# Layer 1 of the first batch over five groups of both rows at once, with two low parts of W1 made by GpSimd

## The chip, the cores and the metric

The kernel runs on one core of one Trainium2 chip. The metric is the device time of one execution in microseconds; lower is better. Engines are named as in the profile: PE is TensorE's matmul, PEld its weight load, DVE VectorE, ACT ScalarE, POOL GpSimd, SP SyncE.

## The reference

Two layers on x of shape (8, 256, 1024), each added to its input. Layer 0 has a full matrix of its own for every batch element, made from a mask; layer 1 has one matrix and a LoRA pair picked by an id.

```python
# layer 0
output = jnp.einsum('bsi,oi->bso', hidden_states, W) + b
sign = (2 * mask - 1).astype(hidden_states.dtype)
diff = jnp.einsum('bsi,bio->bso', hidden_states, sign)
x = x + output + diff * coeff[:, None, None]
# layer 1, SCALING = 2
base_out = jnp.einsum('bti,oi->bto', x, W) + b
lora_h = jnp.einsum('bti,bir->btr', x, lora_As[adapter_mapping])
lora_out = jnp.einsum('btr,bro->bto', lora_h, lora_Bs[adapter_mapping])
x = x + base_out + lora_out * SCALING
```

## The kernel before

**Precision.** Every float32 operand is split into a high part (rounded to float32r by a ScalarE copy) and a low part (the rest, by a subtraction on VectorE or GpSimd), and each product is made of three matmuls: high x high, high x low, low x high. The residual is folded into the weights: GpSimd adds the identity to the diagonal block of W0 and W1 (`w1_diagonal`, L229).

**Batches and tiles.** The eight batch elements follow each other. The contraction of 1024 is cut into KT = 8 blocks k of 128; x and y are held transposed, in four pairs of blocks (`g` in 0 to 3, XG = 4). Layer 0 of batch b writes y in four PSUM banks `y_ps0` to `y_ps3`: for each k, 16 matmuls with the high part of that block of weights (`layer0_high`, L286) and 8 with the low part (`layer0_low`, L296). The weights of block k are made anew for each batch: VectorE adds W0 and 2c times the mask (`weights_sum`, L551), ScalarE takes the high part (`weights_high`, L408), VectorE the low one (`weights_low`, L560). They lie in rings of four blocks, so that mask k + 4 is loaded only after the low part of block k is made.

**Layer 1.** y is split by `y_high` (L426) and `y_low` (L583) out of PSUM. The output's 256 tokens are two rows `s` of 128, and its 1024 columns plus the R = 16 columns of LoRA's A three groups `g` of 352, 344 and 344 columns, one PSUM bank `z_ps0` to `z_ps2` each. `products(b, s, g, k)` (L310) is three matmuls of one group and one block. W1 is split once, in the first batch, by `w1_high` (L414) and `w1_low` (L571); `w1_lo` lies where `w1_raw` lay. Group 0 of a row also yields h, the product with A: `h_high` (L432) and `h_low` (L591) read it, `turn_h` (L344) transposes it on TensorE, `h_copy` (L437) takes it back, and `close_group` (L353) adds h times B and the bias b1 to a group with one matmul. The rows of b1 are split and put into `b_stack` by GpSimd and two DMAs of its queue (L248 to L254); B's low part is `lora_b_low` (L243). `z_copy` (L444) takes a group out of PSUM, and `store` sends a row.

**Order.** There is no planner: each engine's order is written out by hand, and an instruction waits on counting semaphores. `z_done` counts z copies and tells TensorE which bank is free. For batch 0, before: TensorE does `layer0(0)`; then `layer1_first()`, row 0's three groups block by block, each block as soon as its low part is made (`w1_lo_done >= k + 1`); then row 1's group 0 in `y_ps3`, then row 1's group 1. Row 1's group 2 of every batch is left to `layer1_last`, after layer 0 of the next batch. VectorE alternates `w1_low` of eight blocks with `y_low` of four pairs. ScalarE's x block g of batch 0 is split after the weights of block 2g - 1. On SP's queue all loads stand in one order: W0 and mask by turns, x, W1 with LoRA's A and B, then batch 1's x and masks. GpSimd does the diagonals of W0, the b1 rows, the diagonals of W1 (with `lora_a_low(0)`, L237, after the second), then `lora_b_low(0)`.

Of the kernel before, what the change touches and what calls it, by code (L numbers as in the profile page):

```python
# [17 lines left out]
def cond_residual_two_layers(nc, x, coeff, slot_ids, mask, w0, b0, w1, b1, lora_a, lora_b, out):  # L18
# [17 lines left out]
    with ExitStack() as ctx:  # L36
# [69 lines left out]
        w1_hi_done = sem("w1_hi_done")  # L106
        w1_lo_done = sem("w1_lo_done")
        x_hi_done = sem("x_hi_done")
        x_lo_done = sem("x_lo_done")
# [18 lines left out]
        def mask_entry(b, k):  # L128

            return KT * b + k  # L130

        def need(eng, s, n):
# [21 lines left out]
        def z_bank(b, s, g):  # L154

            return y_ps[XG - 1] if (b, s, g) == (0, 1, 0) else z_ps[g]

# [4 lines left out]
        def _(sp):  # L162
# [18 lines left out]
            def load_lora(b):  # L181
# [32 lines left out]
        def _(pool):  # L214
# [30 lines left out]

            pool.wait_ge(w0_diag, KT)
            pool.wait_ge(b1_in, 16)
# [19 lines left out]
        def _(pe):  # L267
            def warm_up(n):
                for _ in range(n):
                    pe.transpose(t_ps[:, 0:P], ident[:], ident[:])  # L270

            def layer0_high(b, k):

                pe.wait_ge(x_lo_done, XG * b + k // PAIR + 1)
                for o in range(KT):
                    if o % HT == 0 and (o == 0 or (b, k) == (0, 0)):
                        pe.wait_ge(wc_hi_done, parts(b, k, o // HT))
                    if k == 0 and o % PAIR == 0:
                        need(pe, y_lo_done, KT * (b - 1) + o + PAIR)
                    if b == 1 and k == 0 and o == KT - PAIR:  # L280

                        pe.wait_ge(z_done, NG + 1)
                    ys = y_ps[o // PAIR][:, (o % PAIR) * T:(o % PAIR + 1) * T]
                    w = wc_hi[:, k % RING, o * P:(o + 1) * P]
                    for n in range(2):
                        pe.matmul(ys, w, x_two[:, k, n, :], start=(k == 0 and o % PAIR == 0 and n == 0),  # L286
                                  stop=False, skip_group_check=True)

            def layer0_low(b, k):

                for o in range(KT):
                    if o % HT == 0 and (o == 0 or (b, k) == (0, 0)):
# [23 lines left out]

            def layer1_first():

                pe.wait_ge(lora_lo_done, 1)
                for k in range(KT):  # L320
                    pe.wait_ge(w1_lo_done, k + 1)
                    pe.wait_ge(y_lo_done, k + 1)
                    for g in range(NG):
                        products(0, 0, g, k)

            def layer1_group(b, s, g, ks=range(KT)):
                if ks[0] == 0:

                    if (b, s, g) != (0, 1, 0):
                        need(pe, z_done, NG * (ST * b + s - 1) + g + 1)  # L330
# [15 lines left out]
            def close_group(b, s, g):  # L346
# [3 lines left out]
                if g == 0:  # L350
# [4 lines left out]
                          start=False, stop=True, skip_group_check=True).then_inc(z_full, 1)  # L355

            def layer1(b):

                for s in range(ST):
                    if b > 0:  # L360
                        layer1_group(b, s, 0)
                        layer1_group(b, s, 1, range(HT))
                        turn_h(b, s)
                        layer1_group(b, s, 1, range(HT, KT))
                        close_group(b, s, 0)
                        close_group(b, s, 1)
                    elif s == 0:
                        layer1_first()
                        layer1_group(0, 1, 0, range(HT))
                        turn_h(0, 0)  # L370
                        layer1_group(0, 1, 0, range(HT, KT))
                        close_group(0, 0, 0)
                        close_group(0, 0, 1)
                    if s == 0 and b > 0:
                        layer1_group(b, 0, 2)
                    if s == 0:
                        close_group(b, 0, 2)
                    if s == 1 and b == 0:
                        layer1_group(0, 1, 1, range(HT))
                        turn_h(0, 1)  # L380
                        layer1_group(0, 1, 1, range(HT, KT))
                        close_group(0, 1, 0)
                        close_group(0, 1, 1)

# [7 lines left out]
            layer0(0)  # L392
            layer1(0)
            for b in range(1, NB):
# [7 lines left out]
        def _(act):  # L402
# [36 lines left out]
            def z_copy(b, s, g):  # L439
                act.wait_ge(z_full, NG * (ST * b + s) + g + 1)  # L440
                if g == 0:
# [5 lines left out]
            def store(b, s, g0=0, g1=NG):  # L447
                act.wait_ge(z_done, NG * (ST * b + s) + g1)
                lo, hi = max(EDGES[g0] - R, 0), EDGES[g1] - R
                act.dma_start(out_v[b, s][:, lo:hi], z_rows[:, s, lo:hi]).then_inc(z_out[s], 16)  # L450

            def lora_a_high(b):
                act.wait_ge(a_in, 16 * (b + 1))
                if b > 0:

                    act.wait_ge(z_full, NG * (ST * b - 1) + 1)
                act.activation(w1_hi[:, :, 0:R], a_raw[:], ACT.Copy).then_inc(lora_hi_done, 1)  # L457
# [25 lines left out]
            y_high(0, 0)  # L483
            w1_high(2)
            y_high(0, 1)
            w1_high(3)
            w1_high(4)
            y_high(0, 2)
            w1_high(5)
            y_high(0, 3)  # L490
            w1_high(6)
            w1_high(7)
            lora_b_high(0)


            for b in range(1, NB + 1):
                a = b - 1
                if a > 0:
                    for g in range(XG):
                        y_high(a, g)  # L500
                if b < NB:
                    for g in range(XG):
                        x_high(b, g)
                if a > 0:
                    z_copy(a - 1, 1, 2)
                    store(a - 1, 1)
                    lora_b_high(a)
                h_high(a, 0)
# [29 lines left out]
        def _(dve):  # L538
# [58 lines left out]


            weights_sum(0, 0, 0)
            x_low(0, 0)  # L600
            weights_sum(0, 0, 1)
            weights_low(0, 0, 0)
            weights_low(0, 0, 1)
            weights_sum(0, 1)
            for k in range(1, KT):
                if k % PAIR == 1 and k < KT - 1:
                    x_low(0, k // PAIR + 1)
                if k < KT - 1:
                    weights_sum(0, k + 1)
                weights_low(0, k)  # L610
            w1_low(0)
# [13 lines left out]
            for b in range(1, NB):  # L625
                a = b - 1
                if a > 0:
                    for g in range(XG):
                        y_low(a, g)
                for g in range(XG):  # L630
# [42 lines left out]
```

## Time and profile before

| what | value |
| --- | --- |
| median of 3 runs | 404.98 us (404.46 to 405.29) |
| the profiled execution's own time | 407.7 us |
| its span, first to last instruction | 405.9 us |
| mean granted TensorE clock | 0.992 |
| busy: PE, PEld | 389.5 us (96%), 385.7 us (95%) |
| busy: DVE, ACT, POOL | 221.0 us, 159.7 us, 39.5 us |
| DMA | 61.80 MB, mean 152 GB/s |

Busy times are of the profiled execution, which took 2.7 us more than the median; 1.8 us of it lie outside the span. An engine that is not the bottleneck may be idle at no cost, so the table alone doesn't tell what sets the time.

### The profile page before, as it was taken

The page shows a single profiled execution, that of the slowest core. Times are in us where ns is not written, and L with a number is a line of the kernel's source. Part 1 is how long each engine was busy: PE and PEld are TensorE (multiplying, and loading weights), DVE is VectorE, ACT ScalarE, POOL GpSimd, SP SyncE. Part 2 cuts the span into 40 slices and gives each one's busy share as a digit, 9 for nine tenths or more (in the row PEclk, how much of TensorE's full clock was granted, in tenths as well). Part 3 has the DMA queues.
Part 4 walks back from the last instruction along what each step waited for, and adds up shares of the span by engine and source line. Part 5 has one row for each costly group of instructions (what it writes and reads, how often), then busy time and mean ns, then how long its engine had stood idle before and what let it go on. Part 6 is the DMA issues. An engine that isn't in the chain of part 4 may idle for free.

```text
span 405.9 us, 6725 instructions
## 1 busy us (share of the span) xinstructions
PE 389.5 (96%) x2782; PEld 385.7 (95%) x2782; DVE 221.0 (54%) x267; ACT 159.7 (39%) x283; POOL 39.5 (10%) x44
## 2 busy tenths in 40 slices
PE   7798797999999999999999999999999999999997
PEld 7688696999999999999999999999999999999996
DVE  2797977616756277525746177553775258460300
ACT  3446834306433353316424064334534164241311
POOL 1236300002000020000200020000200001000200
PEclk9999988999999999999999999999999999999999
DMA  7999808531565126640365216650266413500111
GB/s 250 407 382 333 328 27 271 196 110 53 180 205 174 45 79 207 209 161 33 110 221 199 95 53 191 197 200 16 80 207 219 152 52 111 177 2 2 52 53 52
DMA packets 21056, 61.80 MB, mean 152 GB/s; under 512 B 2698, under 2 KB 3874, under 8 KB 21026
## 3 DMA queue, kind: packets, MB, share of 16 engines
q1 hardware_dynamic: 18064, 52.70, 38.3%
q10 hardware_dynamic: 2898, 8.66, 6.0%
q8 instruction: 22, 0.36, 0.4%
q14 instruction: 8, 0.07, 0.0%
q0 software_dynamic: 64, 0.01, 0.0%
HBM read 52.97 MB, written 8.39 MB: 151 GB/s over the span
## 4 chain that ended last, share of the span: by engine, by line
PE 85%; DMA 4%; DVE 3%; POOL 2%; issue 2%; ACT 1%; SPq 1%; ACTq 0%; DVEq 0%; POOLq 0%
PE z_ps L310 42%; PE y_ps L286 26%; PE y_ps L296 13%; DMA ring<-in_mask 2%; DVE w_lo L571 2%; DMA w_t<-in_w 2%; PE z_ps L353 2%; PE y_ps L310 1%; DVE y_two L583 1%; ACT wc_hi L408 1%; PE t_ps L344 0%; POOL w_t L227 0%; POOL w_raw L232 0%; ACT w_hi L414 0%; POOL b_parts L250 0%
## 5 line engine op out<-in xcount | busy, mean ns | idle before, releaser
L310 PE MATMUL z_ps<-w_hi,y_two 128*128 128x344 f32 (+1 forms) x752 | 189.2, 327 | 4.4 <-DVE w_lo L571 2.7
L310 PEld LDWEIGHTS z_ps<-w_hi,y_two 128*128 128x128 f32 x752 | 133.7, 191 | 6.3 <-DVE w_lo L571 3.6
L286 PE MATMUL y_ps<-x_two,wc_hi 128*128 128x256 f32 x1024 | 133.8, 284 | 2.3 <-ACT wc_hi L408 1.7
L286 PEld LDWEIGHTS y_ps<-x_two,wc_hi 128*128 128x128 f32 x1024 | 127.9, 192 | 3.0 <-issue 1.7
L310 PE MATMUL z_ps<-w_lo,y_two 128*128 128x344 f32 (+1 forms) x376 | 121.8, 324 | 0.0
L560 DVE SCALAR_TENSOR_TENSOR wc_lo<-ring,coeff_neg,wc_hi 128x1024 fp32r<-128x1024 f32 (+1 forms) x65 | 83.1, 1279 | 50.0 <-ACT wc_hi L408 49.2
L408 ACT ACTIVATE wc_hi<-ring,coeff_neg 128x1024 fp32r<-128x1024 f32 (+1 forms) x65 | 74.0, 1138 | 65.6 <-PE y_ps L296 53.6
L551 DVE SCALAR_TENSOR_TENSOR ring<-ring,coeff_two,w_t 128x1024 f32<-128x1024 int32 (+1 forms) x65 | 83.1, 1286 | 6.6 <-DMA ring<-in_mask 6.1
L296 PE MATMUL y_ps<-x_two,wc_lo 128*128 128x256 f32 x512 | 72.2, 284 | 2.5 <-DVE wc_lo L560 2.5
L310 PEld LDWEIGHTS z_ps<-w_lo,y_two 128*128 128x128 f32 x376 | 71.8, 191 | 0.0
L296 PEld LDWEIGHTS y_ps<-x_two,wc_lo 128*128 128x128 f32 x512 | 66.0, 192 | 3.1 <-DVE wc_lo L560 3.1
L583 DVE SCALAR_TENSOR_TENSOR y_two<-y_ps,b_cols,y_two 128x256 fp32r<-128x256 f32 x64 | 26.1, 476 | 65.1 <-ACT y_two L426 65.1
L426 ACT ACTIVATE y_two<-y_ps,b_cols 128x256 fp32r<-128x256 f32 x64 | 24.5, 488 | 67.5 <-PE y_ps L296 67.5
L243 POOL TENSOR_TENSOR b_stack<-b_raw,b_stack 32x1024 fp32r<-32x1024 f32 x8 | 19.1, 2386 | 199.3 <-ACT b_stack L462 199.3
L444 ACT ACTIVATE z_rows<-z_ps 128x344 f32<-128x344 f32 (+1 forms) x47 | 20.0, 459 | 33.7 <-PE z_ps L353 33.7
L591 DVE SCALAR_TENSOR_TENSOR h_rows<-z_ps,h_rows 128x16 fp32r<-128x16 f32 x30 | 3.8, 169 | 47.2 <-ACT h_rows L432 47.2
L576 DVE TENSOR_TENSOR x_two<-x_raw,x_two 128x512 fp32r<-128x512 f32 x32 | 20.2, 684 | 3.2 <-ACT x_two L420 3.2
L432 ACT ACTIVATE h_rows<-z_ps 128x16 fp32r<-128x16 f32 x30 | 3.9, 181 | 39.5 <-PE z_ps L310 39.5
L420 ACT ACTIVATE x_two<-x_raw 128x512 fp32r<-128x512 f32 x32 | 18.1, 665 | 2.7 <-DMA x_raw<-in_x 2.7
L237 POOL TENSOR_TENSOR w_lo<-a_raw,w_hi 128x128 fp32r<-128x128 f32 x8 | 3.7, 462 | 120.0 <-ACT w_hi L457 120.0
L437 ACT ACTIVATE h_stack<-t_ps 66x128 fp32r<-66x128 f32 x16 | 4.4, 273 | 22.3 <-PE t_ps L344 22.3
L571 DVE TENSOR_TENSOR w_lo<-w_raw,w_hi 128x1024 fp32r<-128x1024 f32 x8 | 12.0, 1528 | 1.5 <-ACT w_hi L414 1.5
(35 smaller groups left out, 91.3 us busy)
## 6 DMA issues: line engine op xcount, KB each, us to landing
ring<-in_mask SPq DMA_DIRECT2D x63, 512.0 KB, 3.3
x_raw<-in_x SPq DMA_DIRECT2D x31, 256.0 KB, 5.5
out<-z_rows ACTq DMA_DIRECT2D x15, 512.0 KB, 3.9
w_raw<-in_w SPq DMA_DIRECT2D x8, 512.0 KB, 10.2
w_t<-in_w SPq DMA_DIRECT2D x7, 512.0 KB, 9.1
b_raw<-in_lora_b SPq DMA_DIRECT2D x8, 256.0 KB, 3.5
w_t<-in_w SPq DMA_DIRECT2D x2, 256.0 KB, 4.4
ring<-in_mask SPq DMA_DIRECT2D x2, 256.0 KB, 5.9
```

The costliest lines, as they stand in the source:

```text
L243: pool.tensor_tensor(b_stack[2 * R:LR, :], b_raw[2 * R:LR, :], b_stack[2 * R:LR, :].bitcast(F32), ALU.subtract).then_inc(lora_lo_done, 1)
L286: pe.matmul(ys, w, x_two[:, k, n, :], start=(k == 0 and o % PAIR == 0 and n == 0), stop=False, skip_group_check=True)
L296: ins = pe.matmul(ys, w, x_two[:, k, 0, :], start=False, stop=(k == KT - 1), skip_group_check=True)
L310: ins = pe.matmul(z_bank(b, s, g)[:, 0:EDGES[g + 1] - EDGES[g]], ys[:, k, s * P:(s + 1) * P], w[:, k, EDGES[g]:EDGES[g + 1]], start=(k == ...
L408: act.activation(wc_hi[:, k % RING, lo:hi], sums[:, e % RING, lo:hi], ACT.Identity, bias=coeff_neg[:, b:b + 1]).then_inc(wc_hi_done, 1)
L426: act.activation(y_two[:, b % 2, 0, o, :], y_ps[g][:, (o % PAIR) * T:(o % PAIR + 1) * T], ACT.Identity, bias=b0_cols[:, o:o + 1]).then_inc ...
L444: act.activation(z_rows[:, s, EDGES[g] + lo - R:EDGES[g + 1] - R], z_bank(b, s, g)[:, lo:EDGES[g + 1] - EDGES[g]], ACT.Copy).then_inc(z_do ...
L551: dve.scalar_tensor_tensor(out=sums[:, e % RING, lo:hi], in0=ring[:, e % RING, lo:hi], scalar=coeff_two[:, b:b + 1], in1=w0_t[:, k, lo:hi] ...
L560: dve.scalar_tensor_tensor(out=wc_lo[:, k % RING, lo:hi], in0=sums[:, mask_entry(b, k) % RING, lo:hi], scalar=coeff_neg[:, b:b + 1], in1=w ...
L571: dve.tensor_tensor(w1_lo[:, k, R:R + D], w1_raw[:, k, R:R + D], w1_hi[:, k, R:R + D].bitcast(F32), ALU.subtract).then_inc(w1_lo_done, 1)
L576: dve.tensor_tensor(x_two[:, PAIR * g:PAIR * (g + 1), 1, :], x_raw[:, PAIR * g:PAIR * (g + 1), :], x_two[:, PAIR * g:PAIR * (g + 1), 0, :] ...
L583: dve.scalar_tensor_tensor(out=y_two[:, b % 2, 1, o, :], in0=y_ps[g][:, (o % PAIR) * T:(o % PAIR + 1) * T], scalar=b0_cols[:, o:o + 1], in ...
```

## The change

For batch 0 alone, layer 1 now runs over five groups at once: (0,0), (0,1), (0,2), (1,0) and (1,1), written (row, group). Group (1,0) is held in `y_ps0` and (1,1) in `y_ps1`. They start when `y_low` has read those banks. `layer1_first` does blocks 0 and 1 of four groups, then of the fifth, blocks 2 to 5 of all five, and 6 and 7 group by group; both turns of h stand between the last products of (0,2), and the five closes come at the end, in the order (0,0), (1,0), (1,1), (0,1), (0,2), which `z_place` numbers. Layer 0 of batch 1 begins with output blocks 4 to 7 in its first weight block.

GpSimd makes `w1_lo` of blocks 4 and 7 (`SIDE`), counted by a semaphore of its own; VectorE makes the other six. GpSimd's b1 work moves behind these. SP's queue loads x block 0 first, which ScalarE's queue did before. ScalarE and VectorE have their orders of batch 0 written anew. From batch 2 on the orders are as they were.

```diff
+        SIDE = (4, 7)
+        def w1_split(eng, k):
+            eng.wait_ge(w1_lo_done, k + 1 - sum(j <= k for j in SIDE))
+            need(eng, w1_lo_side, sum(j <= k for j in SIDE))
...
         def z_bank(b, s, g):
-            return y_ps[XG - 1] if (b, s, g) == (0, 1, 0) else z_ps[g]
+            return y_ps[g] if b == 0 and s == 1 and g < 2 else z_ps[g]
+        def z_place(b, s, g):
+            if b == 0:
+                return ((0, 0), (1, 0), (1, 1), (0, 1), (0, 2), (1, 2)).index((s, g)) + 1
+            return NG * (ST * b + s) + g + 1
...
+            load_x(0, 0)
             sp.dma_start(w0_t[:, 0, 0:HALF], w0[0, :, 0:HALF]).then_inc(w0_first, 16)
...
-            pool.wait_ge(w0_diag, KT)
+            w1_diagonal(0)
+            w1_diagonal(1)
+            lora_a_low(0)
+            for k in range(2, KT):
+                w1_diagonal(k)
+            for k in SIDE:
+                pool.wait_ge(w1_hi_done, k + 1)
+                pool.wait_ge(w1_diag, k + 1)
+                pool.tensor_tensor(w1_lo[:, k, R:R + D], w1_raw[:, k, R:R + D],
+                                   w1_hi[:, k, R:R + D].bitcast(F32), ALU.subtract).then_inc(w1_lo_side, 1)
             pool.wait_ge(b1_in, 16)
...
-            w1_diagonal(0)
-            w1_diagonal(1)
-            lora_a_low(0)
-            for k in range(2, KT):
-                w1_diagonal(k)
             lora_b_low(0)
...
+            def outputs(b, k):
+                return [*range(HT, KT), *range(HT)] if (b, k) == (1, 0) else [*range(KT)]
...
-                    if b == 1 and k == 0 and o == KT - PAIR:
-                        pe.wait_ge(z_done, NG + 1)
+                    if b == 1 and k == 0 and o % PAIR == 0 and o < HT:
+                        pe.wait_ge(z_done, z_place(0, 1, o // PAIR))
...
+            def first_products(s, g, ks):
+                for k in ks:
+                    w1_split(pe, k)
+                    pe.wait_ge(y_lo_done, max(k + 1, PAIR * (g + 1) if s == 1 else 0))
+                    products(0, s, g, k)
...
+            def layer1_first():
+                pe.wait_ge(lora_lo_done, 1)
+                for k in range(PAIR):
+                    for s, g in ((0, 0), (0, 1), (0, 2), (1, 0)):
+                        first_products(s, g, [k])
+                first_products(1, 1, range(PAIR))
+                for k in range(PAIR, KT - PAIR):
+                    for s, g in ((0, 0), (0, 1), (0, 2), (1, 0), (1, 1)):
+                        first_products(s, g, [k])
+                for s in range(ST):
+                    first_products(s, 0, range(KT - PAIR, KT))
+                for s in range(ST):
+                    first_products(s, 1, range(KT - PAIR, KT))
+                turn_h(0, 0)
+                first_products(0, 2, [KT - PAIR])
+                turn_h(0, 1)
+                first_products(0, 2, [KT - 1])
+                for s, g in ((0, 0), (1, 0), (1, 1), (0, 1), (0, 2)):
+                    close_group(0, s, g)
...
-            act.dma_start(x_raw[:, 0:PAIR, :], x[0, :, 0:PAIR, :]).then_inc(x_in[0], 16)
...
+            x_high(0, 0)
             for k in range(KT):
-                if k % PAIR == 0:
-                    x_high(0, k // PAIR)
+                if k % PAIR == 1 and k < KT - 1:
+                    x_high(0, k // PAIR + 1)
                 weights_high(0, k)
             w1_high(0)
-            w1_high(1)
             lora_a_high(0)
             act.wait_ge(b0_in, 16)
...
+            for g in range(XG):
+                y_high(0, g)
+                w1_high(g + 1)
+            for k in range(XG + 1, KT):
+                w1_high(k)
             lora_b_high(0)
...
+            for g in range(XG):
+                x_high(1, g)
+            h_high(0, 0)
+            h_high(0, 1)
+            weights_high(1, 0)
+            h_copy(0, 0)
+            h_copy(0, 1)
+            z_copy(0, 0, 0)
+            z_copy(0, 1, 0)
+            z_copy(0, 1, 1)
+            weights_high(1, 1)
+            z_copy(0, 0, 1)
+            z_copy(0, 0, 2)
+            store(0, 0)
+            lora_a_high(1)
+            for k in range(2, KT):
+                weights_high(1, k)
...
+            x_low(0, 0)
             weights_sum(0, 0, 0)
-            x_low(0, 0)
             weights_sum(0, 0, 1)
             weights_low(0, 0, 0)
             weights_low(0, 0, 1)
             weights_sum(0, 1)
+            x_low(0, 1)
             for k in range(1, KT):
...
             w1_low(2)
             w1_low(3)
             y_low(0, 2)
-            w1_low(4)
+            y_low(0, 3)
             w1_low(5)
-            y_low(0, 3)
             w1_low(6)
-            w1_low(7)
...
+            x_low(1, 0)
+            weights_sum(1, 0)
+            h_low(0, 0)
+            h_low(0, 1)
+            for k in range(KT):
+                if k + 1 < XG:
+                    x_low(1, k + 1)
+                step(1, k)
```

## Rows read from the trace of the kernel before

**Rows 1.** The page, parts 1 and 2: busy time, and tenths by slice.
```profile
PE 389.5 (96%) x2782; PEld 385.7 (95%) x2782; DVE 221.0 (54%) x267; ACT 159.7 (39%) x283; POOL 39.5 (10%) x44
...
PE   7798797999999999999999999999999999999997
...
PEclk9999988999999999999999999999999999999999
```
**Rows 2.** The chain of waits in order of time: start us, us, what.
```profile
63.04 0.27 ACT h_rows L432 x2
...
69.10 1.92 PE y_ps L286 x16
71.02 0.96 PE y_ps L296 x8
...
92.14 3.81 PE z_ps L310 x24
...
386.68 0.31 PE z_ps L353 x2
```
**Rows 3.** Timeline of TensorE: start us, us, line, tiles; idle before and releaser.
```profile
8.59 1.22 PE L286 MATMUL y_ps<-x_two,wc_hi 128*128 128x256 f32 x8 [0.66 <-DVE x_two L576]
...
24.04 1.22 PE L296 MATMUL y_ps<-x_two,wc_lo 128*128 128x256 f32 x8 [0.70 <-DVE wc_lo L560]
...
30.34 1.21 PE L296 MATMUL y_ps<-x_two,wc_lo 128*128 128x256 f32 x8 [0.28 <-DVE wc_lo L560]
...
38.38 0.40 PE L310 MATMUL z_ps<-w_hi,y_two 128*128 128x352 f32 x1 [1.07 <-DVE y_two L583]
...
50.46 0.44 PE L310 MATMUL z_ps<-w_hi,y_two 128*128 128x352 f32 x1 [1.93 <-DVE w_lo L571]
...
65.09 0.27 PE L344 MATMUL t_ps<-ident,h_rows 128*66 128x128 f32 x1 [2.81 <-issue]
...
68.90 2.12 PE L286 MATMUL y_ps<-x_two,wc_hi 128*128 128x256 f32 x16
```
**Rows 4.** Stretches of TensorE: stretch us, length, busy, granted clock, DMA share, GB/s.
```profile
36.00:38.00 2.00, 1.31 (x11) 1.00 1.06 400
...
52.00:53.00 1.00, 1.00 (x6) 0.50 0.00 0
...
38.30:68.90 30.60, 23.55 (x120) 0.89 0.62 219
```
**Rows 5.** Timeline of VectorE.
```profile
20.70 0.69 DVE L576 TENSOR_TENSOR x_two<-x_raw,x_two 128x512 fp32r<-128x512 f32 x1 [0.54 <-ACT x_two L420]
...
26.99 0.69 DVE L576 TENSOR_TENSOR x_two<-x_raw,x_two 128x512 fp32r<-128x512 f32 x1 [0.61 <-ACT x_two L420]
...
46.41 0.87 DVE L583 SCALAR_TENSOR_TENSOR y_two<-y_ps,b_cols,y_two 128x256 fp32r<-128x256 f32 x2
...
47.19 3.21 DVE L571 TENSOR_TENSOR w_lo<-w_raw,w_hi 128x1024 fp32r<-128x1024 f32 x1
```
**Rows 6.** Timeline of ScalarE.
```profile
39.64 2.00 ACT L414 ACTIVATE w_hi<-w_raw 128x1024 fp32r<-128x1024 f32 x2
41.53 0.84 ACT L426 ACTIVATE y_two<-y_ps,b_cols 128x256 fp32r<-128x256 f32 x2
```
**Rows 7.** Timeline of SP's queue: when a DMA was issued, and how long that took.
```profile
6.87 0.45 SPq L178 DMA_DIRECT2D x_raw<-in_x  x1
```
**Rows 8.** DMA issues: x block 2, b_raw(1), second b1 row; last: us to landing.
```profile
x_raw<-in_x SPq DMA_DIRECT2D x1, 256.0 KB, 11.1
...
b_raw<-in_lora_b SPq DMA_DIRECT2D x1, 256.0 KB, 3.2
...
b_stack<-b_parts POOLq DMA_DIRECT2D x1, 4.0 KB, 5.6
```
**Rows 9.** Timeline of GpSimd.
```profile
40.49 0.46 POOL L232 TENSOR_TENSOR w_raw<-w_raw,ident 128x128 f32<-128x128 f32 x1 [0.41 <-DMA w_raw<-in_w]
...
43.09 0.66 POOL L232 TENSOR_TENSOR w_raw<-w_raw,ident 128x128 f32<-128x128 f32 x1 [0.74 <-DMA w_raw<-in_w]
...
46.94 2.38 POOL L243 TENSOR_TENSOR b_stack<-b_raw,b_stack 32x1024 fp32r<-32x1024 f32 x1 [3.19 <-ACT b_stack L462]
```

More of the change, by code:

```diff
@@ L270, in warm_up @@
                     pe.transpose(t_ps[:, 0:P], ident[:], ident[:])
+            def outputs(b, k):
+                return [*range(HT, KT), *range(HT)] if (b, k) == (1, 0) else [*range(KT)]
             def layer0_high(b, k):
                 pe.wait_ge(x_lo_done, XG * b + k // PAIR + 1)
-                for o in range(KT):
-                    if o % HT == 0 and (o == 0 or (b, k) == (0, 0)):
+                for o in outputs(b, k):
+                    if (b, k) == (0, 0) and o % HT == 0:
                         pe.wait_ge(wc_hi_done, parts(b, k, o // HT))
+                    if (b, k) != (0, 0) and o == outputs(b, k)[0]:
+                        pe.wait_ge(wc_hi_done, parts(b, k))
                     if k == 0 and o % PAIR == 0:
                         need(pe, y_lo_done, KT * (b - 1) + o + PAIR)
-                    if b == 1 and k == 0 and o == KT - PAIR:
-                        pe.wait_ge(z_done, NG + 1)
+                    if b == 1 and k == 0 and o % PAIR == 0 and o < HT:
+                        pe.wait_ge(z_done, z_place(0, 1, o // PAIR))
                     ys = y_ps[o // PAIR][:, (o % PAIR) * T:(o % PAIR + 1) * T]
@@ L315, in products @@
                     ins.then_inc(h_full, 1)
[L317 to L324, printed above, removed]
+            def first_products(s, g, ks):
[3 more added lines that the diff above has]
+                    products(0, s, g, k)
             def layer1_group(b, s, g, ks=range(KT)):
                 if ks[0] == 0:
-                    if (b, s, g) != (0, 1, 0):
-                        need(pe, z_done, NG * (ST * b + s - 1) + g + 1)
+                    before = (b, 0, g) if s == 1 else (b - 1, 1, g)
+                    if b == 1 and s == 0 and g < 2:
+                        before = (0, 0, g)
+                    pe.wait_ge(z_done, z_place(*before))
                     if s == 0 and g == 0:
@@ L357, in layer1 @@
             def layer1(b):
                 for s in range(ST):
[L360 to L373, printed above, removed]
@@ L374, in layer1 @@
-                    if s == 0 and b > 0:
+                    layer1_group(b, s, 0)
+                    layer1_group(b, s, 1, range(HT))
+                    turn_h(b, s)
+                    layer1_group(b, s, 1, range(HT, KT))
+                    close_group(b, s, 0)
+                    close_group(b, s, 1)
+                    if s == 0:
                         layer1_group(b, 0, 2)
-                    if s == 0:
                         close_group(b, 0, 2)
[L378 to L383, printed above, removed]
@@ L472, in _ @@
             act.wait_ge(coeff_done, 2)
+            x_high(0, 0)
             for k in range(KT):
-                if k % PAIR == 0:
-                    x_high(0, k // PAIR)
+                if k % PAIR == 1 and k < KT - 1:
+                    x_high(0, k // PAIR + 1)
                 weights_high(0, k)
             w1_high(0)
-            w1_high(1)
             lora_a_high(0)
             act.wait_ge(b0_in, 16)
[L483 to L492, printed above, removed]
-            lora_b_high(0)
-            for b in range(1, NB + 1):
+            for g in range(XG):
[3 more added lines that the diff above has]
+                w1_high(k)
+            lora_b_high(0)
+            for g in range(XG):
[15 more added lines that the diff above has]
+                weights_high(1, k)
+            for b in range(2, NB + 1):
                 a = b - 1
-                if a > 0:
-                    for g in range(XG):
-                        y_high(a, g)
+                for g in range(XG):
+                    y_high(a, g)
                 if b < NB:
@@ L604, in _ @@
             weights_sum(0, 1)
+            x_low(0, 1)
             for k in range(1, KT):
-                if k % PAIR == 1 and k < KT - 1:
+                step(0, k)
+                if k % PAIR == 0 and k < KT - PAIR:
                     x_low(0, k // PAIR + 1)
-                if k < KT - 1:
-                    weights_sum(0, k + 1)
-                weights_low(0, k)
             w1_low(0)
@@ L618, in _ @@
             y_low(0, 2)
-            w1_low(4)
+            y_low(0, 3)
             w1_low(5)
-            y_low(0, 3)
             w1_low(6)
-            w1_low(7)
-            for b in range(1, NB):
+            x_low(1, 0)
[6 more added lines that the diff above has]
+                step(1, k)
+            for b in range(2, NB):
                 a = b - 1
-                if a > 0:
-                    for g in range(XG):
-                        y_low(a, g)
+                for g in range(XG):
+                    y_low(a, g)
                 for g in range(XG):
```

18 lines of the change are left out of this document (9 added, 9 removed).

## The prediction

> **What bounds the kernel now.** I read the page first. TensorE is busy for 96% of the span, and the only slices with fewer than nine tenths are the last and five of the first seven; the granted clock dips in the sixth and seventh [rows 1]. So time can be gained at the start only. The chain of waits agrees: from 69.10 on it is matmuls alone, 2.88 us for each block of layer 0 (1.92 and 0.96) and 0.159 us for each matmul of layer 1 (24 in 3.81) [rows 2]. Batches 1 to 7 are that, back to back, and the diff adds and removes no matmul there. All that counts is when layer 0 of batch 1 begins: at 68.90 in TensorE's timeline [rows 3]. From there to the end of the 405.9 us span it is 337.0 us, before and after.
>
> What happens before 68.90? Layer 0 of batch 0 starts at 8.59 and ends at about 37.15 (its last uninterrupted run starts at 30.34: 0.96 + 2 x 2.88 = 6.7 and some tenths of latency), though 8 x 2.88 = 23.0 us of matmuls are in it; it waits for loads and for VectorE's low parts, for the latter 0.70 us at 24.04 and 0.28 at 30.34 [rows 3]. Layer 1 begins at 38.38 and its five groups (120 matmuls) last until 68.90, so 30.5 us for what costs 120 x 0.159 = 19.05 at full clock. The difference has three parts. (a) In the first three groups TensorE spends 9 matmuls = 1.43 us on a block of W1, while VectorE makes W1's and y's low parts more slowly; worst is one w1_low of 3.21 us, before the wait of 1.93 us at 50.46 [rows 3, 5]. (b) Row 1's h is read late: ScalarE takes it at 63.04, behind z copies and layer-0 weights, and TensorE idles 2.81 us at 65.09 before turn_h [rows 2, 3]. (c) After long waits the matmuls run slowly: the granted clock is 0.50, which is 1.2 GHz, from 52 to 53, and 0.89 over the whole stretch, against 1.00 from 36 to 38 [rows 4].
>
> **The change, part by part**, in order of time. Durations are those of the rows.
>
> *Layer 0 of batch 0.* x block 0 moves from ScalarE's queue to the head of SP's, and puts what is behind it back by one issue, 0.45 us [rows 7]. The same bytes are wanted by the same time, so I take 0; the bounds are 0.45 us either way. x_high now stands before the weights of the odd blocks. VectorE idles 0.54 us before x_low(0,2) at 20.70 and 0.61 before x_low(0,3) at 26.99, for ScalarE's x_high in both cases [rows 5], though x block 2 had landed at 6.87 + 11.1 = 17.97 [rows 7, 8]. With x_high made earlier both idles go, unless a mask is then the last to come, and TensorE's waits of 0.70 and 0.28 behind them shrink: nothing to 0.98 us. I take 0.5: layer 0 ends at 36.6 to 36.7 and layer 1 starts at 37.9 (bounds 37.4 and 38.8, with x's issue).
>
> *Layer 1 of batch 0.* TensorE now does 12 matmuls on each of blocks 0 and 1 (then 6 for the fifth group) and 15 on each of blocks 2 to 5: 1.9 and 2.4 us a block. If nothing waits, from 37.9, it wants block 1 at 39.8, block 2 at 42.65, 3 at 45.05, 4 at 47.45, 5 at 49.85, 6 at 52.2, 7 at 52.7. ScalarE now makes w1_high(1) after y_high(0); it needs about 0.75 us for a y pair and 1.0 for a block (0.84 and 2.00 for two, overlapping the next) [rows 6]: with y_high(0) at 36.35, block 1 is split high at 38.1, 2 at 39.8, 3 at 41.5, 4 at 43.2, 7 at 46.1. VectorE follows (1.2 a block, 0.8 a y pair, 0.87 in the row): w1_low(1) ends at 39.3, 0.5 us ahead of its use, w1_low(2) at 41.3, (3) at 42.7, y_low(2) and (3) by 44.3. The margin grows from 0.5 to over 2 us.
>
> *Blocks 4 and 7 on GpSimd.* A 128x1024 subtract on GpSimd is nowhere in the trace. Below it stands the 32x1024 subtract of 2.38 us: more partitions can't shorten it. Above it, 8 of the 128x128 operation of 0.46 us = 3.7 us, its fixed part counted eight times [rows 9]. I take 2.4, since the 32x1024 row has the same length per partition. It starts behind w1_diagonal(7), whose load had landed when it began at 43.09 [rows 9], so at 43.6, and ends at 46.0: in time for 47.45. Meanwhile VectorE is held up. The row that shows it is the w1_low of 3.21 us from 47.19, beside GpSimd's 46.94 to 49.32: it ended 1.1 us after GpSimd did. The two y_low of 46.41, with an input in PSUM, were not stretched [rows 5, 9]. So w1_low(5) ends at 47.2, GpSimd's block 7 runs 47.2 to 49.5, w1_low(6) ends at 50.7. TensorE wants 6 at 52.2 and 7 at 52.7: nothing waits. Had VectorE kept all eight it would have ended at 44.3 + 4 x 1.2 = 49.1, so the handing over is itself a loss of 1.6 us in the chain of low parts, hidden by 1.5 us of margin. The Trainium skill, "Perfetto Trace Analysis", section "Optimizing Scalar/DVE Operations", warns of just that: moving work between VectorE and GpSimd may not help, as they share an SBUF port. The trace agrees, by the 3.21 us row; by the rule the sum stays the same, since the chain of low parts is no longer what ends last.
>
> *What is put behind it on GpSimd.* The b1 rows and lora_b_low(0) now come after block 7. b1's cast and subtract are short but alternate with VectorE's w1_low(6), x_low(1,0) and weights_sum(1,0): done at 51.9, the second b1 DMA is issued at 52.65. It landed 5.6 us after issue in its own row, taken with the DMA engines full (share 1.06 from 36 to 38); the 256 KB of b_raw took 3.2 with them nearly idle [rows 4, 8]: 58.3 or 55.9. I take 55.9, since from 52 the share was 0.00 [rows 4]. lora_b_low runs 53.2 to 55.6. close_group(0,0,0) needs both at 57.1; by the far bound it waits 1.2 us.
>
> *h and the closes.* Row 0's h is complete at 53.2, row 1's at 54.1, and ScalarE and VectorE have nothing ahead of them: h_low(0,1) ends at 54.8, while turn_h comes at 56.0 and 56.6. The 2.81 us wait goes. Five closes take 0.155 each (two in 0.31) [rows 2], the turns 0.1 each by the pitch. The stage: 19.05 + 0.22 + 0.78 = 20.05; 37.9 + 20.05 = 57.95. With no long wait I expect no half clock, and the 0.159 holds throughout.
>
> *Does layer 0 of batch 1 then run?* Its first matmuls go to y_ps2 and 3; y_ps0 and 1 are wanted at 58.9 and copied by 58.6. weights_high(1,0) ends at 55.9, weights_high(1,1), behind three z copies, at 59.6 for 60.8. VectorE can start x_low(1,1) only when lora_b_low is off (55.6): weights_low(1,0) at 58.7 for 59.9, (1,1) at 61.75 for 62.75, (1,2) at 64.8 for 65.6. It holds by 0.8 us. Mask 4, issued at 58.7, is twice b_raw's size: 3.2 to 6.4 us, for a sum at 64.8.
>
> *Sum.* Layer 0 of batch 1 begins at 57.95 instead of 68.90: 10.95 us less. The span becomes 395.0, and the profiled execution's 407.7 us become 396.7; against the median of 404.98 (the profiled one is 2.7 us above it) that is **394.0 us**.
>
> **Rivals.**
>
> A. *GpSimd is slower than 2.4 us.* At 3.7, block 7 is done at 52.2 and w1_low(6) at 53.4, 1.2 us late; the second b1 DMA goes out at 55.4 and lands at 58.6 to 61.0 for a close at 58.3. Together 1.5 to 3.9 us back: 395.5 to 397.9. For it: 128 partitions at this length are not measured. Against it: the fixed time in the 128x128 row.
>
> B. *b1 becomes the last wait.* GpSimd in time, the DMA at 5.6 us: 1.2 us, 395.2. For it: the only row of this DMA. Against it: full DMA engines then, idle ones now. The Trainium skill, "SBUF — State Buffer", section "SBUF: two separate sides", adds that a DMA issued from GpSimd's queue can starve for descriptors under some VectorE instructions; no row here separates that from full engines, and by it the time would be this rival's.
>
> C. *VectorE is late in layer 0 of batch 1*, where I count 0.8 us of margin: one more lock of GpSimd's length, 2.4 us, less 0.8 and some of it made up later, is about 1 us, 395.0.
>
> D. *Slower.* GpSimd's subtract goes by elements: 4 x 2.38 = 9.5 us. Then block 4 is done at 53.1, block 7 at 63.8, w1_low(6) at 65.0, b1 lands at 70.3 to 72.8, and layer 0 of batch 1 begins at 71.1 to 73.6, 2.2 to 4.7 us later than now: 407.2 to 409.7. It decides from 7.2 to 8.4 us per block, where 44.8 + 2t + 6.5 to 9.0 + 0.8 = 68.9. Against it: the 128x128 row makes 3.7 a ceiling.
>
> E. *The change doesn't do what it says*: the waits come back elsewhere in full, 405.0. Only several of the above at once would do that.
>
> **How the numbers follow.** My forecast 0.60 (its own range 393.2 to 394.9: 0.9 us late or 0.8 early), A 0.13, B 0.12, C 0.09, D 0.03, E 0.03. The range, 393.2 to 396.6, takes in the forecast, B, C and the lower half of A. Faster, same and slower are told apart at 0.2%, 0.8 us, about what a measurement of this kernel can tell: faster 0.94, same 0.03, slower 0.03.
>
> **What would show it.** Layer 1's first matmul at 37.4 to 38.8; its 120 matmuls in 19 to 20 us with a granted clock of 1.00; GpSimd's two subtracts at 2.4 us, w1_low(5) or (6) stretched to over 2 us with no wait on TensorE; turn_h without a wait; the first matmul of batch 1 near 58. The prediction is wrong if a close waits for b1, if TensorE waits at block 6 or 7 or drops to half clock, or if layer 0 of batch 1 waits for wc_lo.

## Result, and the profile after

The changed kernel takes 398.1 us (median of 4 runs, 396.88 to 398.73) against 404.93 for the kernel before (4 runs): ratio 0.9828, 95% interval 0.9803 to 0.9854. It is 6.8 us faster. I had forecast 394.0, range 393.2 to 396.6, so the direction was right and the gain overestimated by 4 us. The profiled execution is one of the four: 397.99 us, span 396.2.

The page of the changed kernel, parts 1 and 2:

```profile
PE 386.6 (98%) x2782; PEld 384.5 (97%) x2782; DVE 220.9 (56%) x265; ACT 159.8 (40%) x283; POOL 47.1 (12%) x46
...
PE   5899999999999999999999999999999999999997
...
PEclk9699999999999999999999999999999999999999
```

Beside [rows 1]: the holes of slices 4, 5 and 7 are gone, the one in slice 1 is larger (5 tenths instead of 7), and the dip of the granted clock has moved from slices 6 and 7 to slice 2. GpSimd has 7.6 us more to do.

The chain of waits of the changed kernel, the part that answers to [rows 2]:

```profile
57.20 0.11 PE t_ps L371
57.30 0.47 PE z_ps L336 x3
57.77 0.26 PE t_ps L371
58.03 0.56 PE z_ps L336 x3
58.59 0.15 PE z_ps L380
58.75 0.31 PE y_ps L380 x2
59.06 0.32 PE z_ps L380 x2
59.37 1.93 PE y_ps L312 x16
```

ScalarE's reading of h is no longer in it: the turns of h and the five closes follow each other on TensorE, and layer 0 of batch 1 comes straight behind.

TensorE's timeline of the changed kernel, which answers to [rows 3]:

```profile
1.52 5.56 PE L290 MATMUL t_ps<-ident 128*128 128x128 f32 x30 [1.52 <-POOL ident L233]
10.15 3.75 PE L312 MATMUL y_ps<-x_two,wc_hi 128*128 128x256 f32 x16 [3.07 <-ACT wc_hi L441]
...
18.60 1.21 PE L322 MATMUL y_ps<-x_two,wc_lo 128*128 128x256 f32 x8 [0.83 <-DVE wc_lo L604]
...
24.96 1.22 PE L322 MATMUL y_ps<-x_two,wc_lo 128*128 128x256 f32 x8 [0.33 <-DVE wc_lo L604]
...
38.79 0.40 PE L336 MATMUL z_ps<-w_hi,y_two 128*128 128x352 f32 x1 [0.95 <-DVE y_two L627]
...
58.43 0.32 PE L380 MATMUL z_ps<-b_stack,h_stack 66*128 66x336 f32 x1
...
59.21 2.09 PE L312 MATMUL y_ps<-x_two,wc_hi 128*128 128x256 f32 x16
```

Stretches of the same kernel, as in [rows 4]:

```profile
10.00:13.00 3.00, 2.85 (x13) 0.50 1.00 383
52.00:53.00 1.00, 1.00 (x8) 1.00 0.00 0
38.79:59.21 20.42, 20.42 (x127) 1.00 0.63 233
```

Layer 1's 120 matmuls with turns and closes take 20.42 us without a hole and with a granted clock of 1.00; before they took 30.5. That is the whole of the gain: layer 0 of batch 1 begins at 59.21 instead of 68.90, 9.69 us earlier, and the span fell by 9.7. But the first matmul came at 10.15, not near 8.6, behind a wait of 3.07 us, and the granted clock is 0.50 there; layer 1 began at 38.79, not at 37.9.

GpSimd's two subtracts, and then VectorE's two beside them (timelines of the changed kernel, to hold against [rows 5, 9]):

```profile
44.46 2.43 POOL L270 TENSOR_TENSOR w_lo<-w_raw,w_hi 128x1024 fp32r<-128x1024 f32 x1
46.94 3.30 POOL L270 TENSOR_TENSOR w_lo<-w_raw,w_hi 128x1024 fp32r<-128x1024 f32 x1
```
```profile
45.25 2.72 DVE L615 TENSOR_TENSOR w_lo<-w_raw,w_hi 128x1024 fp32r<-128x1024 f32 x1
...
47.89 3.43 DVE L615 TENSOR_TENSOR w_lo<-w_raw,w_hi 128x1024 fp32r<-128x1024 f32 x1
```

They take turns. GpSimd's first has nothing ahead of it: 2.43 us. VectorE's, dispatched at 45.25, ends at 47.97, 1.1 us after GpSimd's end at 46.89; GpSimd's second ends at 50.24, 2.3 after VectorE's first; VectorE's second at 51.32, 1.1 after that. Each waits out the other's instruction. The Trainium skill, "SBUF — State Buffer", section "Who interferes with whom", has it so: a VectorE instruction with two SBUF inputs contends with a GpSimd one that reads SBUF, and one of them waits for the whole of the other. The trace agrees, with these four rows.

### The profile page after: what moved, and what is told of

It is laid out like the page before. It is cut to its first block, busy times and chain, and to the rows that moved or that the text cites. A ratio compares the mean times of both kernels' runs of the same rounds, so it can differ in the third digit from the quotient of the medians.

```text
span 396.2 us, 6760 instructions
## 1 busy us (share of the span) xinstructions
PE 386.6 (98%) x2782; PEld 384.5 (97%) x2782; DVE 220.9 (56%) x265; ACT 159.8 (40%) x283; POOL 47.1 (12%) x46
## 4 chain that ended last, share of the span: by engine, by line
PE 93%; DMA 3%; SPq 1%; DVE 1%; issue 1%; POOL 0%; ACT 0%; DVEq 0%; ACTq 0%
PE z_ps L336 44%; PE y_ps L312 29%; PE y_ps L322 15%; DMA w_t<-in_w 3%; PE y_ps L336 2%; PE z_ps L380 2%; DVE wc_lo L604 1%; PE t_ps L371 0%; POOL w_t L243 0%; SPq L183 0%; DVE ring L595 0%; SPq L189 0%; SPq L193 0%; ACT y_two L459 0%; DVE y_two L627 0%
## 5 line engine op out<-in xcount | busy, mean ns | idle before, releaser
L336 PE MATMUL z_ps<-w_hi,y_two 128*128 128x344 f32 (+1 forms) x736 | 183.7, 324 | 1.0 <-DVE y_two L627 1.0
L312 PE MATMUL y_ps<-x_two,wc_hi 128*128 128x256 f32 x1024 | 135.3, 286 | 3.1 <-ACT wc_hi L441 3.1
L312 PEld LDWEIGHTS y_ps<-x_two,wc_hi 128*128 128x128 f32 x1024 | 129.6, 195 | 3.3 <-issue 3.3
L336 PEld LDWEIGHTS z_ps<-w_hi,y_two 128*128 128x128 f32 x736 | 129.5, 188 | 1.8 <-issue 1.1
L336 PE MATMUL z_ps<-w_lo,y_two 128*128 128x344 f32 (+1 forms) x368 | 118.3, 321 | 0.0
L322 PE MATMUL y_ps<-x_two,wc_lo 128*128 128x256 f32 x512 | 73.0, 286 | 1.2 <-DVE wc_lo L604 1.2
L336 PEld LDWEIGHTS z_ps<-w_lo,y_two 128*128 128x128 f32 x368 | 69.4, 189 | 0.0
L620 DVE TENSOR_TENSOR x_two<-x_raw,x_two 128x512 fp32r<-128x512 f32 x32 | 21.1, 707 | 7.1 <-ACT x_two L453 7.1
L253 POOL TENSOR_TENSOR w_lo<-a_raw,w_hi 128x128 fp32r<-128x128 f32 x8 | 4.7, 582 | 104.4 <-ACT w_hi L490 104.4
L380 PE MATMUL z_ps<-b_stack,h_stack 66*128 66x344 f32 (+1 forms) x46 | 12.3, 320 | 0.0
```

What stands on the lines that cost most here:

```text
L336: ins = pe.matmul(z_bank(b, s, g)[:, 0:EDGES[g + 1] - EDGES[g]], ys[:, k, s * P:(s + 1) * P], w[:, k, EDGES[g]:EDGES[g + 1]], start=(k == ...
L380: pe.matmul(z_bank(b, s, g)[:, lo:EDGES[g + 1] - EDGES[g]], h_stack[0:KS, s * P:(s + 1) * P], b_stack[0:KS, EDGES[g] + lo - R:EDGES[g + 1] ...
L620: dve.tensor_tensor(x_two[:, PAIR * g:PAIR * (g + 1), 1, :], x_raw[:, PAIR * g:PAIR * (g + 1), :], x_two[:, PAIR * g:PAIR * (g + 1), 0, :] ...
```

## The experiments

A time is the median of a kernel's runs. The experiments ran in three groups, each on a chip of its own and with the kernel before beside it; its medians there are 405.66, 405.81 and 405.59 us.

**The kernel before, once more** (no edit).

> The kernel before, once more, for the spread of its executions. Theory S (the sum was made against an unusually slow execution): most executions have a span near 403.2, 2.7 under the profiled 405.9, and the profiled one if it is one of these shows shorter half-clock stretches or starts layer 0 of batch 1 near 66 instead of 68.90. Theory X (only the start of the changed kernel is late): spans of 405 to 406 are common in the kernel before, and the median difference of the two kernels on this chip is near 8 to 9 us.

Measured: 405.16 us over 12 runs, ratio 0.9995 (0.9976 to 1.0014). The profiled execution takes 404.36, span 402.6. Its rows, TensorE's timeline first, then the stretch that ran at half clock in [rows 4]:

```profile
38.11 0.40 PE L310 MATMUL z_ps<-w_hi,y_two 128*128 128x352 f32 x1 [1.07 <-DVE y_two L583]
...
50.19 0.43 PE L310 MATMUL z_ps<-w_hi,y_two 128*128 128x352 f32 x1 [2.06 <-DVE w_lo L571]
...
63.29 0.27 PE L344 MATMUL t_ps<-ident,h_rows 128*66 128x128 f32 x1 [2.81 <-issue]
...
65.60 2.08 PE L286 MATMUL y_ps<-x_two,wc_hi 128*128 128x256 f32 x16
```
```profile
52.00:53.00 1.00, 1.00 (x8) 1.00 0.00 0
```

The same waits of 2.06 and 2.81 us, and no half clock behind them: layer 0 of batch 1 begins at 65.60, 3.3 us before that of [rows 3], and 15.4 us after the wait at 50.19 instead of 18.4. So whether the clock falls after such a wait changes from one execution to the next. Every run comes with a mean granted clock, and over the 61 runs of the kernel before in these three groups the times go with it:

| mean granted clock | runs | mean us | range us |
| --- | --- | --- | --- |
| 1.000 | 12 | 404.17 | 403.42 to 405.07 |
| 0.996 | 30 | 405.46 | 404.77 to 406.35 |
| 0.992 | 18 | 406.58 | 405.59 to 407.51 |
| 0.987 | 1 | 409.09 | |

A step of 0.004 in the mean clock goes with 1.1 to 1.3 us, which I read as one stretch at half clock; a typical execution then has about one. The profile that I worked from had two, behind the two waits (0.992), and, at 407.7, was slower than any of these 18. The first stretch is in [rows 4]; the second stands in the same view:

```profile
66.00:67.00 1.00, 1.00 (x5) 0.50 1.02 418
67.00:68.00 1.00, 1.00 (x5) 0.50 1.04 410
```

Theory S holds for the reference: I had made the sum against an execution 2.7 us above the median. Both theories' times for it (403.2, or 405 to 406 of span) hit only a part of the spread.

**The changed kernel, once more** (no edit).

> The changed kernel once more, for the spread on the same chip. Theory X: the first matmul is again near 10.1, the last of the five groups' closes near 59.2, 398. Theory S: the first matmul moves by 1 us or more between the two profiles of one kernel.

Measured: 397.83 us over 5 runs (397.51 to 399.29). The first matmul is at 10.14, layer 1 starts at 38.66 and layer 0 of batch 1 at 59.08: 20.42 us again. Theory X, as far as these two profiles go; the table below has others that start earlier.

**x block 0 on ScalarE's queue again.**

```diff
-            load_x(0, 0)
...
             act.dma_start(coeff_all[:], coeff).then_inc(coeff_in, 16)
+            act.dma_start(x_raw[:, 0:PAIR, :], x[0, :, 0:PAIR, :]).then_inc(x_in[0], 16)
```

> The changed kernel with x block 0 loaded by ScalarE's queue again, its only edit. Theory X (x at the head of SP's queue holds back coeff, W0 and the masks by 1.3 us): the first matmul comes back from 10.15 to about 8.7, layer 1 starts at 37.5 to 37.9, time 396.8, 1.3 us under the changed kernel. Theory S (the start varies from execution to execution, the queue has no part in it): no difference beyond 0.4 us, the first matmul anywhere from 8.6 to 10.2.

Measured: 396.79 us over 5 runs (396.54 to 398.14), ratio to before 0.9793 (0.9766 to 0.9821): 1.2 us under the changed kernel, whose nine runs have a median of 397.99. Layer 1 starts at 37.45. The first matmul did not come back: it stands at 10.63, though this kernel's coeff is there at 3.77. Here x_low stands before the first sum on VectorE and x lands late, at about 7.6. So there are two things at the start, and only one of them costs time that shows (the experiment "The best start" removes the other). GpSimd's wait for coeff, changed kernel, then this one:

```profile
6.11 0.25 POOL L237 TENSOR_SCALAR coeff_two<-coeff_all 128x8 f32<-128x8 f32 x1 [4.64 <-DMA coeff_all<-in_coeff]
```
```profile
3.77 0.25 POOL L236 TENSOR_SCALAR coeff_two<-coeff_all 128x8 f32<-128x8 f32 x1 [2.31 <-DMA coeff_all<-in_coeff]
```

The sum of weight block 2 starts when mask 2 has landed. VectorE's timeline, changed kernel, then this one:

```profile
16.07 1.28 DVE L595 SCALAR_TENSOR_TENSOR ring<-ring,coeff_two,w_t 128x1024 f32<-128x1024 int32 x1 [1.30 <-DMA ring<-in_mask]
```
```profile
14.72 1.28 DVE L595 SCALAR_TENSOR_TENSOR ring<-ring,coeff_two,w_t 128x1024 f32<-128x1024 int32 x1 [0.98 <-DMA ring<-in_mask]
```

With x at the head of SP's queue mask 2 is late by 1.3 us in this profile. Over the profiles of all the runs:

| x block 0 on | orders | profiles | coeff used at | sum 2 starts | layer 1 starts |
| --- | --- | --- | --- | --- | --- |
| ScalarE's queue | before | 4 | 3.77 to 3.82 | 14.53 to 14.83 | 38.05 to 38.38 |
| ScalarE's queue | changed | 3 | 3.77 to 3.78 | 14.45 to 14.72 | 37.18 to 37.45 |
| SP's queue | changed | 5 | 5.80 to 6.45 | 14.89 to 16.07 | 37.53 to 38.79 |
| SP's queue | before | 1 | 6.43 | 15.22 | 38.82 |

coeff is late each time, by 2.0 to 2.7 us, mask 2 by anything from nothing to 1.6. The new orders bring the start of layer 1 forward by 0.8 us (means of the first two lines: 38.18 and 37.35), and x's place takes 0.1 to 1.6 back. From the start of sum 2 to that of layer 1 it is 23.3 to 23.6 us in the five profiles with the old orders and 22.6 to 23.1 in the eight with the new: when mask 2 lands sets when layer 1 starts, and VectorE's two idles before x_low [rows 5] are gone. In the kernel of this experiment the first of these rows reads:

```profile
20.02 0.95 DVE L620 TENSOR_TENSOR x_two<-x_raw,x_two 128x512 fp32r<-128x512 f32 x1
```

With x on SP's queue the start still varies by 1.3 us from profile to profile, between kernels whose edits, but for the warm-up's, touch nothing that early. So theory S is right about a part of it: the queue makes a late start possible, but doesn't bring it every time. What decides it is not shown.

**All eight low parts of W1 on VectorE.**

```diff
-        SIDE = (4, 7)
+        SIDE = ()
...
             y_low(0, 3)
+            w1_low(4)
             w1_low(5)
             w1_low(6)
+            w1_low(7)
```

> The changed kernel with all eight low parts of W1 on VectorE. My reading (the handing over to GpSimd is hidden either way): the chain of low parts ends at 45.3 + 4 x 1.2 = 50.1 instead of 51.3, TensorE doesn't wait, within 0.3 us of the changed kernel. The rival (VectorE needs the relief): a wait of 1 us or more at block 4 or 5.

Measured: 397.11 us over 5 runs (396.78 to 398.03). Layer 1 starts at 37.57 and layer 0 of batch 1 at 58.00: 20.43 us, as with GpSimd's help, and no wait inside. The difference in time, more than the 0.3 us that I allowed, lies in the start (its sum 2 starts at 14.89). VectorE's timeline of the changed kernel, then of this one:

```profile
45.25 6.08 DVE L615 TENSOR_TENSOR w_lo<-w_raw,w_hi 128x1024 fp32r<-128x1024 f32 x2
```
```profile
43.89 5.23 DVE L615 TENSOR_TENSOR w_lo<-w_raw,w_hi 128x1024 fp32r<-128x1024 f32 x4
```

Two blocks beside GpSimd's subtracts take VectorE longer than four without them. The rival falls.

**Both edits together.** The diff is the two above.

> Both edits on the changed kernel: x block 0 on ScalarE's queue and all eight low parts of W1 on VectorE. Theory H (the offload to GpSimd is hidden and worth nothing; x's queue is worth about 1 us): the same as with x on ScalarE's queue alone, 396.8, and 1 us under the changed kernel; layer 1 takes 20.4 us from its first matmul to the end of its closes. Rival (the low parts matter once layer 1 starts earlier): a wait of over 0.5 us in layer 1 and 397.5 or more.

Measured: 396.65 us over 5 runs (396.55 to 396.83), ratio to before 0.9772 (0.9752 to 0.9792). Layer 1 runs from 37.43 to 57.85, 20.42 us. Theory H, though x's place is priced only roughly: with GpSimd's help it is worth 1.2 us by the medians (396.79 against 397.99), without it 0.5 (396.65 against 397.11, on another chip), and the single runs overlap.

**The offload alone, in the kernel before.** Blocks 4 and 7 to GpSimd, the wait of `layer1_first` counted accordingly, nothing else.

```diff
             for k in range(2, KT):
                 w1_diagonal(k)
+            for k in (4, 7):
+                pool.wait_ge(w1_hi_done, k + 1)
+                pool.wait_ge(w1_diag, k + 1)
+                pool.tensor_tensor(w1_lo[:, k, R:R + D], w1_raw[:, k, R:R + D],
+                                   w1_hi[:, k, R:R + D].bitcast(F32), ALU.subtract).then_inc(w1_lo_side, 1)
+            pool.wait_ge(w1_lo_side, 2)
             lora_b_low(0)
...
-            w1_low(4)
             w1_low(5)
             y_low(0, 3)
             w1_low(6)
-            w1_low(7)
```

> The kernel before with only the offload: GpSimd makes low parts 4 and 7, VectorE the other six, orders as they were. Theory L (the two engines exclude each other): GpSimd's 2.4 us per block cost VectorE more than the 1.2 it saves, except where VectorE reads y from PSUM; TensorE's waits for w1_lo, 2.7 us in the kernel before, stay or grow, time 404.5 to 407. Rival R (the offload relieves VectorE): the waits fall by 2 us, 402.5 to 403.5.

Measured: 407.45 us over 8 runs, ratio 1.0034 (1.0007 to 1.0060): not faster, slightly slower, and 0.45 us above theory L's range. TensorE's timeline:

```profile
41.52 0.43 PE L317 MATMUL z_ps<-w_hi,y_two 128*128 128x352 f32 x1 [0.31 <-DVE w_lo L579]
47.09 0.40 PE L317 MATMUL z_ps<-w_hi,y_two 128*128 128x352 f32 x1 [2.45 <-issue]
```

The waits of 0.59, 0.21 and 1.93 us became 0.31 and 2.45, in sum the same; the longer one is at block 4, whose subtract GpSimd starts at 43.56 and ends at 46.99, 3.43 us with its turn behind VectorE. Six of the eight runs have a mean granted clock of 0.992 or less, of the fifteen of the kernel before on that chip seven, which may be the rest of the difference; that isn't isolated. Theory L holds, R falls.

**h of row 1 read earlier, in the kernel before.**

```diff
                 z_copy(a, 0, 1)
+                if a == 0:
+                    h_high(0, 1)
...
                 step(b, 0)
+                if a == 0:
+                    h_low(0, 1)
                 step(b, 1)
```

(the later h_high and h_low are left out for batch 0).

> The kernel before with only h of row 1, batch 0, read earlier: h_high behind the second z copy on ScalarE, h_low behind the first weights_low on VectorE. My reading: the 2.81 us wait before turn_h goes and with it the second stretch of half clock where there was one; the z copy of group 2 is late by 0.3 us. 2.5 to 4.0 us under the kernel before: 401.5 to 403. Rival (the wait moves to the next z copy or to weights_high): under 1 us gained.

Measured: 403.01 us over 6 runs (401.55 to 404.88), ratio 0.9932 (0.9905 to 0.9959): 2.8 us under the kernel before. The wait at turn_h is gone, and a part of it came back one step later, at the close (TensorE's timeline):

```profile
63.74 0.42 PE L353 MATMUL y_ps<-b_stack,h_stack 66*128 66x336 f32 x1 [1.29 <-ACT h_stack L437]
...
64.15 2.08 PE L286 MATMUL y_ps<-x_two,wc_hi 128*128 128x256 f32 x16
```

64.15 against 65.60 for the kernel before without half clock: layer 0 of batch 1 starts 1.45 us earlier. The rest of the 2.8 fits the clock (all six runs at 0.996 or above), but that split is argued from the table above, not isolated.

**Three blocks on GpSimd, in the changed kernel.**

```diff
-        SIDE = (4, 7)
+        SIDE = (4, 6, 7)
...
             w1_low(5)
-            w1_low(6)
```

> The changed kernel with GpSimd making blocks 4, 6 and 7 (one more subtract of 2.4 us in front of b1). By the rows of the changed kernel: GpSimd's third subtract ends at 52.5 to 53 for a use at 53.8, b1's second DMA is issued near 54.8 and lands 1.7 us later, lora_b_low ends at 57.8, ahead of the first close at 58.4. Then no more than 0.3 us slower. Rival B (b1 and lora_b_low become the last wait): the first close waits 0.5 us or more, and the half clock may come with it: 398.5 to 400.

Measured: 400.28 us over 4 runs (399.29 to 401.82), 2.3 us over the changed kernel. TensorE's timeline, then GpSimd's:

```profile
48.69 0.40 PE L336 MATMUL z_ps<-w_hi,y_two 128*128 128x352 f32 x1 [0.35 <-issue]
54.87 0.40 PE L336 MATMUL z_ps<-w_hi,y_two 128*128 128x352 f32 x1 [0.68 <-issue]
61.29 0.40 PE L380 MATMUL z_ps<-b_stack,h_stack 66*128 66x336 f32 x1 [1.45 <-POOL b_stack L259]
```
```profile
46.17 8.60 POOL L270 TENSOR_TENSOR w_lo<-w_raw,w_hi 128x1024 fp32r<-128x1024 f32 x3
...
57.84 3.30 POOL L259 TENSOR_TENSOR b_stack<-b_raw,b_stack 32x1024 fp32r<-32x1024 f32 x1
```

The three waits add up to 2.48 us, about what the time grew by. Rival B came true here, not through b1's DMA but through lora_b_low behind it, which ends at 61.14; half clock did not come with it. In the changed kernel lora_b_low ends at 56.02 for a close at 58.43, a margin of 2.4 us. It ends 5.1 us later here, and not all of that is the third subtract: GpSimd's first one starts 1.7 us later (46.17 against 44.46), because the last block of W1 landed later in this execution. The remaining 3.4, the third subtract with the turns between it and VectorE's work, would still be 1.0 more than the margin, and the fastest of the four runs is 1.3 us over the changed kernel's median.

**x at the head of SP's queue, in the kernel before.** The reverse of the edit above.

> The kernel before with only x block 0 at the head of SP's queue. Theory X: coeff lands at 6.1 to 6.5 instead of 3.8, the first sum starts at 7 or later, mask 2 lands up to 1.3 us later, layer 1 starts 0.2 to 1.2 us later: 405.5 to 407, slower than the kernel before on this chip by about 1 us. Theory N (the later starts of the changed kernel come from its other orders): no difference.

Measured: 406.91 us over 12 runs against 405.59, ratio 1.0014 (0.9985 to 1.0042): inconclusive by time, because the clock's spread of 4 us covers it. Its profile is the last line of the table above: coeff late, layer 1 at 38.82, 0.4 to 0.8 us later than with x on ScalarE's queue. Theory X by the profile alone.

**The best start.** x on ScalarE's queue, all low parts on VectorE, and on VectorE

```diff
-            x_low(0, 0)
             weights_sum(0, 0, 0)
+            x_low(0, 0)
```

> The changed kernel with x block 0 on ScalarE's queue, all low parts of W1 on VectorE, and VectorE's first sum ahead of x_low(0,0), as in the kernel before. Then the first matmul is at 8.6 and runs at full clock. If the end of layer 0 hangs on the masks' landing, the time stays at 396.6 within 0.3; if it hangs on the first block's start, 395.5 or less.

Measured: 396.47 us over 6 runs (396.36 to 396.72), ratio 0.9769 (0.9731 to 0.9807). The first matmul is back at 8.69, and all six runs have a granted clock of 0.999 or more; layer 1 starts at 37.18 and lasts 20.41. Against 396.65 that is no difference to rely on: the end of layer 0 hangs on the masks. It is the fastest kernel of the study, 1.5 us under the changed one's nine runs, and its own runs lie within 0.4 us.

**60 warm-up transposes instead of 30, in the changed kernel.**

> The changed kernel with 60 warm-up transposes in place of 30, so that TensorE is busy until its first real matmul. The granted clock stays at 1.00 from 10 to 15 us. If the half clock of the first block costs something, the time falls by 0.3 to 1 us; if TensorE waits for weights_low anyway, no difference beyond 0.3 us.

Measured: 397.46 us over 6 runs (396.98 to 398.38). The granted clock is 1.00 from 8 us on. Its median is 0.5 us under the changed kernel's, inside the spread of both; its profile has an early start of sum 2 (14.94) and of layer 1 (37.53), which is enough to explain that. Whether the half clock of the first block costs anything stays open; by these medians it is no more than about half a microsecond.

## Why the prediction was wrong, point by point

**The step that failed is the last one, "against the median of 404.98 (the profiled one is 2.7 us above it) that is 394.0".** I took a gain read from one execution, 10.95 us, off the median. But that execution had 2.7 us more than the median one, and the change removes much of just that. Two stretches at half clock cost 3.0 us there (18.4 against 15.4 us between the wait at 50 and layer 0 of batch 1), where by the table a typical execution has one of 1.1 to 1.3: some 1.5 to 1.9 of the 2.7. Another 0.3 is the start of layer 1 (38.38 against 38.11), and 0.6 that the median of three runs, 404.98, was low: over the 61 runs on three chips it is 405.61. These parts are sized by two profiles and the table, no closer; executions of one mean clock still differ by 1.6 to 1.9 us. A kernel that has no waits in that stretch lands at the same place from either: from 407.7 to 397.99 the profiled pair gained 9.7 us, while the two second profiles, 404.36 and 397.83, are 6.5 apart. So the forecast should have stayed with the profiled execution's own sum, 396.7, and its bounds. That step is 2.7 of the 4.1 us.

**The second error is the start, "I take 0; the bounds are 0.45 us either way".** Forecast 37.9, measured 38.79. The outer bound, 38.8, only just held. I priced x's new place by one issue of SP's queue. In this profile coeff comes 2.3 us later than with x on ScalarE's queue, and mask 2 1.3. The other half of that step was right: the idles before x_low went, TensorE's waits of 0.70 and 0.28 behind them became 0.33 and nothing, and the new orders bring layer 1 forward by 0.8 us (0.5 forecast).

**The third is small:** 20.42 us for the stage instead of 20.05. The first matmul takes 0.23 us to the next instead of 0.16, the turns and closes 2.18 with their six matmuls instead of 1.95.

With these, 396.7 + 0.9 + 0.4 = 398.0, and the profiled execution took 397.99. The signs that I had named for layer 1 all came: its first matmul just inside the bounds, no wait and no half clock in the stage. So it was the step from the profile to the median that failed, with the price of the start behind it, and not the mechanism of layer 1. No rival had the number for its reason either: A reached up to 397.9, but through a slow GpSimd.

**What bounds the kernel:** right. From layer 0 of batch 1 to the end it is 337.0 us in both profiles (405.9 - 68.90; 396.2 - 59.21).

**Parts (a), (b), (c) of layer 1's 30.5 us:** (a) and (b) right, since their waits are gone; reading h early alone is worth 2.8 us. (c) was read rightly from the row, and wrongly taken to be there in every execution.

**GpSimd at 2.4 us:** right, 2.43. Rivals A and D fall. **The handing over is a loss, hidden by margin:** right, shown three ways: equal with it and without it in the changed kernel, no better in the kernel before, slower with one block more (a part of that was a late load).

**b1:** I took 3.2 us to land; the row says 1.7, below both bounds, so rival B was further off than I gave it; lora_b_low, which I had behind it, ends 2.4 us ahead of its close. **Rival C:** layer 0 of batch 1 had no wait.

DMA issues of the changed kernel, out of the window from 49 to 56.5 (last column us to landing):

```profile
b_stack<-b_parts POOLq DMA_DIRECT2D x2, 4.0 KB, 1.7
```

**The range** was built on the mechanisms' prices alone. The largest uncertainty, how the profiled execution differs from the others, had no place in it.

## What to carry to other kernels

Ask first how the profiled execution stands to the median, and which of its rows the difference lies in. If the change removes those rows, take the gain off the profiled execution's own time, and not off the median as well. In these traces VectorE's and GpSimd's subtracts with two inputs in SBUF wait out each other; moving two of them across cost VectorE more than it freed (6.08 us for the two left to it, 5.23 for all four), and was harmless only while neither engine was what TensorE waited for. The first few DMAs of a kernel are worth a trial of their own: x's place in the queues there moved the loads behind it by up to 1.6 us.

## What the runs showed of the hardware

After the same two waits of about 2 and 2.8 us, TensorE's granted clock fell to 0.50 in one execution and stayed at 1.00 in another of the same kernel; of 61 runs 12 have a mean clock of 1.000. Moving one 256 KB load from ScalarE's queue to the head of SP's delayed a 4 KB load at the head of ScalarE's queue from 3.8 to between 5.8 and 6.5 us, in all six profiles. The second of the two small DMAs of GpSimd's queue landed in 5.6 us with the DMA engines full, and the two in 1.7 with them idle; other work ran on VectorE in the two cases, and no run separates that from the full engines.
